# The narrow attention layer in two 64-row halves of the array, with paired banks and one maximum instruction per pair

## The reference, cut to what matters

```python
xn = rmsnorm(x, norm_w)
q  = xn @ wq                     # 2048 x 256: 16 heads of 16 columns
k, v = cond @ wk, cond @ wv      # 1601 x 64: 4 heads of 16 columns
probs = softmax(q_h @ k_g.T / 4) # 2048 x 1601 for each of the 16 heads
out = concat(probs @ v_g) @ wo   # 2048 x 256, added to x
```

## Time and profile before

| | us |
|---|---|
| three runs | 4593.92, 4595.06, 4601.59 |
| span of the profiled execution (the page gives no other time for it) | 4597.9 |
| PE busy | 4495.0 (98%) |
| DVE busy | 3081.4 (67%) |
| ACT busy | 2309.8 (50%) |
| POOL busy | 2827.0 (61%) |

### The profile page before, as it was taken

How to read it: one execution, slowest core, us unless ns; L and a number is a source line. 1 busy time by engine, 2 the same in 40 slices (tenths; PEclk the granted TensorE clock), 3 DMA queues, 4 the chain that set the end, 5 groups by cost and what they waited for, 6 DMA issues and landing times.

```text
span 4597.9 us, 56871 instructions
## 1 busy us (share of the span) xinstructions
PE 4495.0 (98%) x20657; PEld 2841.8 (62%) x20657; DVE 3081.4 (67%) x5037; ACT 2309.8 (50%) x4121; POOL 2827.0 (61%) x1365
## 2 busy tenths in 40 slices
PE   8999999999999979999999999999999999999999
PEld 7888866666656545555556666666656656665664
DVE  3321467777777678777846777777767677777776
ACT  3222455554555436666655555555555545554553
POOL 0000368898889711111036988898884888898886
PEclk9999999999999979999999999999999999999999
DMA  4555832221222021011234222222216212222220
GB/s 151 180 187 166 283 86 63 68 69 45 67 64 52 13 39 16 12 15 16 57 97 123 67 59 53 64 69 49 56 45 223 63 37 67 64 69 53 59 48 29
DMA packets 124633, 349.68 MB, mean 76 GB/s; under 512 B 28085, under 2 KB 46005, under 8 KB 113338
## 3 DMA queue, kind: packets, MB, share of 16 engines
q1 hardware_dynamic: 124352, 346.04, 28.4%
HBM read 191.31 MB, written 120.31 MB: 68 GB/s over the span
## 4 chain that ended last, share of the span: by engine, by line
PE 92%; DVE 6%; issue 1%; DMA 1%; ACT 0%; SPq 0%; POOL 0%; DVEq 0%; ACTq 0%
PE ST L989 13%; PE SS L970 12%; PE ST L990 12%; PE OA L1000 12%; PE OB L1000 11%; PE ST L1134 5%; PE OA L1142 4%; PE SS L1120 3%; DVE acc L1581 3%; PE OB L1120 1%; PE SS L1009 1%; DVE mpart L1560 1%; PE ST L1065 1%; PE ST L1066 1%; PE ST L1067 1%
## 5 line engine op out<-in xcount | busy, mean ns | idle before, releaser
L870 POOL TENSOR_TENSOR acc<-acc,P 128x1024 f32<-128x1024 f32 x912 | 2216.6, 2460 | 299.5 <-DVE acc L1587 286.3
L1321 ACT ACTIVATE P<-ST 128x512 f32<-128x512 f32 (+1 forms) x2496 | 1463.7, 597 | 1260.8 <-PE ST L990 1117.5
L1560 DVE TENSOR_REDUCE mpart<-SS 128x1 f32<-128x400 f32 (+1 forms) x3072 | 1629.7, 570 | 669.7 <-PE SS L970 594.4
L989 PE MATMUL ST<-QX,KX 128*128 128x512 f32 (+1 forms) x2496 | 1024.2, 410 | 3.5 <-DMA QS<-mrow 1.7
L970 PE MATMUL SS<-KS,QS 68*128 68x400 f32 (+1 forms) x3072 | 977.6, 352 | 14.7 <-DMA QS<-stq 8.3
L990 PE MATMUL ST<-QS,KS 69*128 69x512 f32 (+1 forms) x2496 | 990.1, 397 | 0.0
L970 PEld LDWEIGHTS SS<-KS,QS 68*128 68x128 f32 x3072 | 583.9, 190 | 191.3 <-DVE xacc L1611 23.9
L989 PEld LDWEIGHTS ST<-QX,KX 128*128 128x128 f32 (+1 forms) x2496 | 463.9, 186 | 360.2 <-issue 272.8
L1000 PE MATMUL OA<-P,Vp 128*64 128x512 f32 (+1 forms) x2496 | 658.3, 606 | 0.0
L1000 PE MATMUL OB<-P,Vp 128*64 128x512 f32 (+1 forms) x2496 | 641.3, 592 | 0.0
L1420 ACT ACTIVATE PG<-ST 128x512 f32<-128x512 f32 (+1 forms) x832 | 426.3, 618 | 213.3 <-PE ST L1134 213.1
(11 more groups left out here) (250 smaller groups left out, 4492.3 us busy)
## 6 DMA issues: line engine op xcount, KB each, us to landing
q_parts<-stq SPq DMA_DIRECT2D x96, 512.0 KB, 5.2
QX<-q_parts SPq DMA_DIRECT2D x96, 512.0 KB, 11.2
KX<-k_parts SPq DMA_DIRECT2D x48, 801.0 KB, 9.1
QS<-q_parts SPq DMA_DIRECT2D x45, 512.0 KB
R<-R SPq DMA_DIRECT2D x360, 64.0 KB, 2.0
v_tiles<-sv SPq DMA_DIRECT2D x24, 832.0 KB, 6.5
Vp<-v_tiles SPq DMA_DIRECT2D x24, 832.0 KB, 7.1
k_parts<-skh SPq DMA_DIRECT2D x48, 400.5 KB, 4.9
```

The source lines that it names most:

```text
L870: gp.tensor_tensor(out, out, P[0:k, slot(H, t), q, :], ALU.add).then_inc(pool_a, 1)
L989: pe.matmul(bank, KX[H % 2][:, t * 128:t * 128 + k], QX[H % 2][:, q], start=True, stop=False)
L1321: act.activation(P[0:k, slot(H, t), j, :], ST[n % 3][0:k, :], ACT.Exp, scale=SCALE).then_inc(act_p, 1)
L1560: dve.tensor_reduce(mpart[H % 2][:, i // len(KCH), c:c + 1], SS[RING_AT["s", H, i] % 3][:, 0:w], AX.X, ALU.max).then_inc(dve_ss, 1)
```

## The change

The strips of 32 rows become strips of 16: q high, q low, q high over k high, k high, k low, which is 48 rows (GROWS), and with the row of maxima 49. The fourth partial product, low times low, is dropped. This stack stands twice, in rows 0 to 48 and in rows 64 to 112. The upper half of GQ holds the query blocks j = 0 and 2 (query tiles 0-3 and 8-11), the lower half the blocks 1 and 3, each packed into the first 1024 columns. So two products, one on each half of the rows, stand back to back in the list. The first pass takes one key chunk for two query tiles that way: 32 pairs for a head. The four banks become two pairs of neighbouring banks in one tensor, S4, and one maximum instruction reads both banks of a pair. All other items of the ring (q, o, z, m) take a pair too; an output item is now both 128-column blocks of one j, with one addition of 1024 columns. A pair may start once the item two places before it was read. The values move from bank OA to OB. Scores are issued two at a time, followed by the pairs of the first pass. GQ takes six DMAs per head instead of four, the maxima two instead of one, KG 24 in all instead of 16; the clearing of GQ is gone.

```diff
-MROW = 3 * QD + D1
+GROWS = 3 * D1
+HALF = 64
+GPAIRS = SUNITS // 2
+HP = HU // 2
+def group_pairs(h, g, w):
+    if g >= ROW_STEP:
+        v = w + (JQ // 2 * len(PV[ROW_STEP + 1]) if g > ROW_STEP else 0)
+        return 2, (part(GPAIRS, v, HP) if h + 2 < HEADS else range(0))
+    v = JQ // 2 * sum(len(PV[i + 1]) for i in range(g)) + w
+    if h + 1 >= HEADS:
+        return 1, range(0)
+    return 1, (part(GPAIRS, v, BEFORE_ROW // 2) if h == 0 else part(GPAIRS, HP - BEFORE_ROW // 2 + v, HP))
+def group_o_item(h, g, w):
+    return 2 * g + w // 2 if h % GROUPS == 1 and h > GROUPS and g < 2 and w % 2 == 0 else None
+def group_q_item(h, g, w):
+    return 2 * g + w // 2 if h % QHEADS == QHEADS - 2 and h + 2 < HEADS and g < 2 and w % 2 == 0 else None
...
-        SS = [bank(f"SS{i}") for i in range(3)]
-        OA, OB = bank("OA"), bank("OB")
-        GS = SS + [OB]
+        S4 = ctx.enter_context(nc.psum_tensor("S4", [128, 4, 512], F32))
+        OB = bank("OB")
+        SS, OA = [S4[:, i, :] for i in range(3)], S4[:, 3, :]
...
         def wait_group_ring(eng, at):
-            if at < len(GS):
+            if at < 2:
                 return
-            kind, n, i = GRING[at - len(GS)]
+            kind, n, i = GRING[at - 2]
+        def group_bank(kind, n, i, e=0):
+            return S4[:, GRING_AT[kind, n, i] % 2 * 2 + e, :]
...
             def group_s(h, i):
-                pe.matmul(GS[at % 4][:, 0:w], GQ[h % 3][0:MROW, qt * 128:(qt + 1) * 128],
-                          KG[h % GROUPS][0:MROW, o:o + w], start=True, stop=True).then_inc(gpe_s, 1)
+                for half in range(2):
+                    k = slice(HALF * half, HALF * half + GROWS)
+                    last = pe.matmul(group_bank("s", h, i, half)[:, 0:w], GQ[h % 3][k, qt * 128:(qt + 1) * 128],
+                                     KG[h % GROUPS][k, o:o + w], start=True, stop=True)
+                last.then_inc(gpe_s, 1)
             def group_scores(h, t, j):
                 wait(pe, gact_p, n - 2)
-                pe.matmul(ST[n % 3][0:k, :], KG[h % GROUPS][0:MROW + 1, t * 128:t * 128 + k],
-                          GQ[h % 3][0:MROW + 1, j * 512:(j + 1) * 512], start=True, stop=True).then_inc(gpe_st, 1)
+                r = slice(HALF * (j % 2), HALF * (j % 2) + GROWS + 1)
+                pe.matmul(ST[n % 3][0:k, :], KG[h % GROUPS][r, t * 128:t * 128 + k],
+                          GQ[h % 3][r, j // 2 * 512:(j // 2 + 1) * 512], start=True, stop=True).then_inc(gpe_st, 1)
...
             def group_s_max(h, i):
-                dve.tensor_reduce(mpart[h % 2][:, i // len(KCH), c:c + 1], GS[GRING_AT["s", h, i] % 4][:, 0:w],
+                dve.tensor_reduce(mpart[h % 2][:, qt:qt + 9:8, c:c + 1], group_banks("s", h, i)[:, :, 0:w],
                                   AX.X, ALU.max).then_inc(gdve_ss, 1)
...
             def group_head(h):
                 for g in range(STEPS):
-                    for u, (on, t, j) in enumerate(units(h, g)):
-                        group_scores(h + on, t, j)
+                    both = units(h, g)
+                    for w in range(len(both) // 2):
+                        for on, t, j in both[2 * w:2 * w + 2]:
+                            group_scores(h + on, t, j)
+                        ahead, tiles = group_pairs(h, g, w)
...
                         for i in tiles:
                             group_s(h + ahead, i)
                     pe.wait_ge(gact_p, HU * h + JQ * (PV[g][-1] + 1))
```

More of the change, by code:

```diff
@@ L189, in group_order @@
 def group_order():
-    out = [("q", 0, j) for j in range(JQ)] + [("s", 0, i) for i in range(SUNITS)] + [("m", 0, 0)]
+    out = [("q", 0, j) for j in range(JQ)] + [("s", 0, i) for i in range(GPAIRS)] + [("m", 0, 0)]
     for h in range(HEADS):
         for g in range(STEPS):
-            for u in range(len(units(h, g))):
-                if takes_row(h, g, u):
+            for w in range(len(units(h, g)) // 2):
+                if takes_row(h, g, w):
                     out.append(("m", h + 1, 0))
[L197 to L201, removed]
+                if group_o_item(h, g, w) is not None:
+                    out.append(("o", h // GROUPS - 1, group_o_item(h, g, w)))
+                if group_q_item(h, g, w) is not None:
+                    out.append(("q", h // QHEADS + 1, group_q_item(h, g, w)))
+                ahead, tiles = group_pairs(h, g, w)
                 out += [("s", h + ahead, i) for i in tiles]
@@ L204, in group_order @@
                 out.append(("z", h - 1, 0))
-    return out + [("z", HEADS - 1, 0)] + [("o", ROUNDS - 1, i) for i in range(8)]
+    return out + [("z", HEADS - 1, 0)] + [("o", ROUNDS - 1, j) for j in range(JQ)]
 GRING = group_order()
@@ L724, in load_gwq, with group_k @@
                             .then_inc(gd_wq, 16)
[L726 to L730, removed]
+            def group_k(g):
+                for i, r in enumerate((0, 0, 1)):
+                    for half in range(2):
+                        to = HALF * half + i * D1
+                        sp.dma_start(words(KG[g][to:to + D1, :]), dKG[r, g * QD:g * QD + D1, :]).then_inc(gd_k, 16)
             def group_q(h):
@@ L792, in group_layer @@
                 for b in range(3):
-                    sp.wait_ge(gd_q[b], 64 * len(range(b, HEADS, 3)))
+                    sp.wait_ge(gd_q[b], 96 * len(range(b, HEADS, 3)))
                 for H in range(HEADS, HEADS + 3):
@@ L885, in group_layer @@
                 for k in KG:
-                    gp.memset(words(k[3 * QD:4 * QD, :]), 1.0).then_inc(pool_ones, 1)
-                gp.wait_ge(pool_ones, GROUPS)
-                for q in GQ:
-                    gp.memset(words(q[:, :]), 0.0).then_inc(pool_ones, 1)
+                    for half in range(2):
+                        gp.memset(words(k[HALF * half + QD:HALF * half + 2 * QD, :]), 1.0).then_inc(pool_ones, 1)
                 for h in range(HEADS):
@@ L1192, in group_layer @@
                     group_project(0, j)
-                pe.wait_ge(gd_k, 16 * 4 * GROUPS)
-                for i in range(SUNITS):
+                pe.wait_ge(gd_k, 16 * 6 * GROUPS)
+                for i in range(GPAIRS):
                     group_s(0, i)
@@ L1204, in group_layer @@
                 group_sums(HEADS - 1)
-                for i in range(8):
-                    group_output(ROUNDS - 1, i)
+                for j in range(JQ):
+                    group_output(ROUNDS - 1, j)
             for l in range(BIG):
@@ L1412, in group_take_o @@
                 wait(act, gpool_on, 4 * (h - 1))
-                copy(Oraw[:, h % 2, :], OA[:, :]).then_inc(gact_o, 1)
+                copy(Oraw[:, h % 2, :], OB[:, :]).then_inc(gact_o, 1)
             def group_exps(h, t, j):
@@ L1425, in group_head @@
                         group_take_z(h - 1)
-                    for u, (on, t, j) in enumerate(units(h, g)):
-                        group_exps(h + on, t, j)
-                        if group_q_item(h, g, u) is not None:
-                            group_hi(h // QHEADS + 1, group_q_item(h, g, u))
+                    both = units(h, g)
+                    for w in range(len(both) // 2):
+                        for on, t, j in both[2 * w:2 * w + 2]:
+                            group_exps(h + on, t, j)
+                        if group_q_item(h, g, w) is not None:
+                            group_hi(h // QHEADS + 1, group_q_item(h, g, w))
                 group_take_o(h)
@@ L1738, in group_layer @@
                 group_reciprocals(HEADS - 1)
-                for i in range(8):
-                    group_add(ROUNDS - 1, i)
-                    if i % 2 == 1 and i > 1:
-                        split_x(1, (i - 3) // 2)
+                for j in range(JQ):
+                    group_add(ROUNDS - 1, j)
+                    if j > 0:
+                        split_x(1, j - 1)
             for l in range(BIG):
```

117 lines of the change are left out of this document (61 added, 56 removed).

## The result

The changed kernel takes 4712.48 us (median of four runs, 4704.78 to 4720.84) against 4598.33 us for the kernel before, run on the same chip: a ratio of 1.0249, with an interval of 1.0229 to 1.0269. It is about 114 us slower. I had forecast 4630 in a range of 4578 to 4672, so the sign was right, and the size and the range were wrong. The profiled execution has a span of 4703.2 us against 4597.9.

The account below looks back on a forecast made before the run. DVE together with the ring of four banks was taken to end the step, although PE looks full. Longer heads (22.9), output projection (9) and smaller terms made +35 us on 4597.9, so 4633, forecast as 4630, range 4578 to 4672.

Parts of the forecast that it names:

- The paced ring: Ordinary narrow-layer step: scores waiting for exponentials delay maxima pairs in a two-deep ring; 6.25 us, +0.25 on 6.00; chance 0.58.
- the step of the output projection: Steps with output items in the narrow layer: 9.28 us now, end at 11.05 after, +1.77; six such steps, +9.
- the step behind the sums: Step after the sums in each head: ACT starts later because the copy of the sums goes ahead; +0.45 us.
- score 5: In an ordinary step, it waits for exponential 2, starts at 2.27, and the third maxima pair follows at 2.51.
- pacing is absent: Rival for the ordinary step: second scores do not hold back maxima, DVE alone ends it at 5.88; 4580 us, chance 0.14.
- rows do not overlap: Rival: a pair's second maximum product comes 0.18 later on two links, step 6.53; about 4663 us, chance 0.15.
- the sign given: Sign of being right: a pair's second product starts 0.1 us or less behind the first.
- PE's gain: Ordinary step: overlapping pairs take about 1.8 us of work off PE, which is cover and not path.
- the short step: Short step of each head: holds the transpose between products on half the rows; +0.06 us.
- The clock falls to 1.2 GHz in steps with less work: Rival: values add 1.85 us and products 0.8 in each of 84 steps; over 4820 us, chance 0.05.
- head 15: Evidence on the clock: it stayed at 1.00 there with 3.8 us of PE work in 5.49, against 3.7 in 6.25 after.
- the forecast's own terms: Sum: heads 1 to 13 +22.9, head 14 +1.5, head 0 +0.3, output +9, q +1.3, start -1.5 and +1, final +0.5; +35 us.

Follow-up runs that it names:

- e3: Kernel before with operands on 48 and 49 rows, in upper and lower half in turn; single banks, ring of four and old order kept: 4682.66 us, ratio 1.0182.
- e4: Changed kernel with each pair of maximum products issued twice into the same banks: 4689.06 us, ratio 1.0196.
- e1: Changed kernel with the pairs of maximum products between the two scores of a pair, except in q projection steps: 4751.6 us, ratio 1.0334.
- e7: e2 with the order of e1, pairs of maxima between the two scores of a pair: 4651.82 us, ratio 1.0113.
- e8: Kernel before with scores issued two at a time, followed by the maximum products of both, nothing else changed: 4627.9 us, ratio 1.0055.
- e2: Changed kernel with the old operands over 112 and 113 rows; its pairs, ring of two, order and paired maximum kept: 4668.26 us, ratio 1.0151.
- e5: Kernel before with scores and maxima on 49 and 48 rows, all in the upper half of the array: 4793.07 us, ratio 1.0421.
- e9: e5 with its products run over 112 and 113 rows, the added query rows holding zeros: 4598.23 us, ratio 0.9995.
- e10: Changed kernel with both halves filled by rows of zeros to 63 and 64 rows: 4673.99 us, ratio 1.0155.
- e6: Changed kernel with the first pair of maximum products of each step issued three times: 4694.28 us, ratio 1.0204.

## Why the prediction was wrong

**The steps that held.** The page's 98% for PE was rightly not taken as the bound: e3 takes work off PE and leaves the step at 5.98, and e4 adds work to PE and the kernel gets faster. The paced ring was right in its main links: 6.23 for 6.25, a paired maximum at 0.99 for 0.98, following the next at 28.87 / 32 = 0.90 for 0.89 in the chain of waits,

```profile
1656.68 28.87 DVE mpart L1701 x32
```

the step of the output projection at 11.13 for 11.05, and the step behind the sums at 7.28 against 6.85 before, +0.43 where I had taken +0.45. That a waiting score is the cause is shown twice. In the changed kernel score 5 starts at 2.22, where the rival "pacing is absent" needed it before 1.9, and e1, which takes that score out of the way of the maxima, has no idle time of DVE inside the step; e1 and e7 put the price at 0.19 and 0.20 a step. e8 does not show it: its 0.24 comes from another link, the late first maximum.

That the two halves of the rows overlap is shown by the first lines of the step at 2210.57: the first maxima product starts 0.34 after the first score, as before, but with two scores ahead of it. The rival "rows do not overlap" is out. The Trainium skill (TensorEngine Tiling (Array Packing), Theoretical Speedup) promised up to twice the rate, and the trace agrees for these products.

The weight loads of a pair run side by side too: the last pair's two loads take 0.19 us at 2214.56, as one does, and 0.30 on the full rows of e2. I had left both open. Where the pair stands behind a score that waited, the sign given did not hold: its second product, on the half that the score is using, starts 0.33 behind the first (2211.82 and 2212.15), not 0.1 or less. DVE starts on that pair at 1.97, close to the 1.93 worked out, because the sum had put the whole pair 0.24 behind the score.

PE's gain was worth nothing but cover, as forecast. One small term had the wrong sign: the short step was to be 0.06 longer and is 0.18 shorter (3.60 against 3.78), so an ordinary head at full clock is 1.44 longer and not 1.76.

**The step that failed** is the last rival: "The clock falls to 1.2 GHz in steps with less work", with a chance of 0.05 and a price of over 200 us. Two things were wrong in it. First the comparison. I held 3.7 us of products in a step of 6.25 against 3.8 in one of 5.49 in head 15, found them near each other, and put the clock aside. That counted the time of products only. The products of head 15 span 113 rows, and those of the changed kernel 49, and e5 against e9 shows what that makes: same times at full clock, same columns, 0.76 against 1.00. Head 15 was no evidence for the case. No row of the trace of before holds a long stretch of products on few rows, which was itself a reason for a higher chance and a wider range.

Second the price. I priced it as if the clock fell in every step (84 times 2.65). It fell in some steps of each head: the changed kernel ran at 0.86 over the layer. In a head of 44.4 us two of the seven steps were hit, and they lasted 7.60 and 8.09 (2197.07 - 2188.98) for 6.23, that is 1.4 and 1.9 more, not 2.65. Of the 103.6 us lost in the layer the forecast's own terms make about 31, put in at their measured sizes where there are any (13 heads by 1.44, six steps of the output projection by 1.6 beyond that, 1.1 for the q projection, and unmeasured the forecast's 1.5 for head 14 and its 0.3 for the rest), where I had said 35; the clock makes the other 70 or so. At a full clock the forecast of 4630 would so have been about right, and the right sign is no luck; but it is not what made most of the 114 us. This split is worked out and not measured by a kernel with this order and a full clock throughout; e10, with part of the clock back, is 38 us faster than the change and has the one head of 41.18.

The range then failed because it reached 4672, up to the rows that do not overlap, and left the clock out altogether. A fallen clock in part of the steps would have stood between 4633 and 4820, and that is where the time came out.

**Where the time went**, by parts: the order alone costs 29 us (e8), order, ring of two and paired maximum on full rows 69 us (e2), and half rows on the old order 83 us (e3). They do not add up to 114, at least in part because the overlap helps the new order (6.60 to 6.23) and had nothing to give to the old one, where PE was not the limit.

**The gaps.** e5 shows that gaps are not needed for the clock to fall. e4 and e6, which fill idle time, raise it to 0.97 and 0.91 all the same. So both count; how the two are weighed against each other is open, and so is why the clock falls in a given step and not in its neighbour. In e3 the halves overlap and the clock is at 0.87, while in e5 nothing overlaps and it is at 0.76: that fits with more rows being at work at once, but it is argued from these two alone.

## What to carry to other kernels

Ahead of a change that puts a long stretch of products on fewer rows of the array, compare the rows that they span, not just their time, with stretches whose granted clock is known; if there are none, price a fall in part of the steps, and keep it in the range. When the clock has fallen, filling the unused rows with zeros can be tried before anything else: it cost nothing in a step at full clock here, and brought 195 us in one kernel and 38 us in another. When work comes off an engine that looks full, find by step which links end it: here PE, DVE and ACT lay within half a microsecond, so relieving one was worth 0.15 us a step at best. The order of an engine's list is worth as much: a waiting score ahead of maxima that could run cost 0.2 a step (e1, e7), and a second score ahead of the first maximum 0.24 (e8).

## What the runs showed of the hardware

- The granted clock depends on the rows that products span, zeros included: 0.76 on 48 and 49 rows and 1.00 on 112 and 113, from the same list with the same waits (busy 599.46 and 598.31 of 600 us); filling halves from 48 to 63 rows took it from 0.86 to 0.93. The Trainium skill (TensorE: Matmul & The Clock Gate, What's actually happening) says that the clock is set by "how busy the PE has been recently". By that alone e5, busy for 99.9% of the time, would have kept the full clock; the measurement decides against busy time as the only thing.
- Products on the two halves of the rows overlap wholly: two take no longer than one did, 0.18 us for a pair of maxima products and 0.34 for two first scores. Products on the same half still follow one another: 0.33 us from a score of 512 columns to the maxima product behind it.
- One maximum instruction over two banks of 400 lasts 0.99 us, two single ones at their pitch take 0.97. Back to back, a paired one takes 0.90. Half as many instructions on DVE so brought little, since single ones, 0.565 long, already follow each other at 0.483.
- A kernel with a shorter step at full clock can be slower as a whole (e1 with 6.04 against 6.23, 39 us slower), while the same edit on full rows is faster (e7 against e2, 16 us). A step's length at full clock can't be compared without the granted clock beside it.
